# GpSimd no longer waits for VectorE's w_lo in front of x_lo and the identity addition into W2

## The reference

```
x = x + (x @ weight[subject].T + bias[subject])            # L0: 8 subjects, 512 x 512
x = x + rotate(x, amplitudes ** dt, frequencies * dt)      # L1: pairs of tokens are turned and scaled
x = x + (x @ W[category] + b[category])                    # L2: 64 categories, 512 x 512
h = relu(x @ W1[lang] + b1[lang])                          # L3: one of 10 languages, 512 -> 128 -> 512
x = x + layernorm(x + h @ W2[lang] + b2[lang]) * gamma[lang] + beta[lang]
```

## Time and profile before

| what | value |
|---|---|
| median of three runs | 1252.36 us |
| the profiled execution | 1252.07 us |
| its span, first to last instruction | 1250.2 us |
| mean granted TensorE clock, share of full speed | 0.995 |
| TensorE (PE) busy | 94% |
| VectorE (DVE) busy | 79% |
| GpSimd (POOL) busy | 63% |
| ScalarE (ACT) busy | 47% |
| HBM traffic over the span | 232 GB/s |

### The profile page before, as it was taken

One profiled execution on the slowest core, in us unless ns is written; L12 is line 12 of the kernel. 1 busy time (PEld: TensorE's weight loads), 2 busy tenths in 40 slices (PEclk: granted clock), 3 DMA queues, 4 the chain that ended last, 5 costly groups with the idle time before them and its releaser, 6 DMA issues.

```text
span 1250.2 us, 28648 instructions
## 1 busy us (share of the span) xinstructions
PE 1175.2 (94%) x5902; PEld 886.8 (71%) x5902; DVE 990.5 (79%) x1465; ACT 582.2 (47%) x923; POOL 783.6 (63%) x792
## 2 busy tenths in 40 slices
PE   2799999999989999999999999999999999999996
PEld 1667767777767777677777677767776777767774
DVE  3488888888888788888788788788888888778887
ACT  2345445444444444545444445454444544444542
POOL 3966656656666657656666566666656666755654
PEclk9999999999999999999999999999999999999999
DMA  6967776776776678667768676776677687867771
GB/s 246 418 206 237 230 242 204 247 235 203 251 256 221 208 248 277 222 205 232 254 199 268 225 231 205 248 259 219 224 243 251 199 251 240 271 214 222 238 225 59
DMA packets 96410, 291.75 MB, mean 233 GB/s; under 512 B 11584, under 2 KB 11712, under 8 KB 78272
## 3 DMA queue, kind: packets, MB, share of 16 engines
q1 hardware_dynamic: 96192, 289.52, 70.6%
HBM read 255.93 MB, written 33.55 MB: 232 GB/s over the span
## 4 chain that ended last, share of the span: by engine, by line
PE 53%; DVE 24%; issue 12%; DVEq 8%; DMA 1%; POOL 1%; SPq 0%; POOLq 0%; ACT 0%; ACTq 0%
DVE w_lo L630 11%; PE ps_l L752 9%; PE ps_l L784 9%; PE ps_y L813 9%; PE ps_l L747 6%; DVE ps_y L658 5%; DVE stats L660 5%; PE ps_x3T L794 4%; DVEq L202 3%; DVEq L205 3%; PE ps_l L774 3%; PE ps_l L737 3%; PE ps_l L778 3%; PE ps_mix L763 3%; PE ps_hT L804 3%
## 5 line engine op out<-in xcount | busy, mean ns | idle before, releaser
L381 POOL TENSOR_TENSOR x_lo<-x_in,x_hi 128x512 fp32r<-128x512 f32 x128 | 165.5, 1293 | 360.1 <-DVE w_lo L630 356.8
L630 DVE TENSOR_TENSOR w_lo<-w_in,w_hi 128x1024 fp32r<-128x1024 f32 x256 | 304.1, 1229 | 0.0
L486 ACT ACTIVATE w_hi<-w_in 128x1024 fp32r<-128x1024 f32 x256 | 255.2, 1045 | 7.9 <-PE ps_l L778 4.7
L451 ACT ACTIVATE ps_diag<-ident,cos 128x128 f32<-128x128 f32 x128 | 47.6, 372 | 382.1 <-DVE mix L604 381.8
L784 PE MATMUL ps_l<-w_lo,x2T_hi 128*128 128x512 f32 x512 | 174.5, 424 | 19.5 <-DVE w_lo L630 15.2
L405 POOL TENSOR_TENSOR x<-x,beta_sb 128x512 f32<-128x512 f32 x128 | 162.9, 1272 | 28.9 <-POOL x3b L398 28.7
L763 PEld LDWEIGHTS ps_mix<-mix,x 128*128 128x128 f32 x1024 | 133.7, 191 | 63.1 <-issue 58.6
L737 PE MATMUL ps_l<-w_hi,x_hi 128*128 128x512 f32 x512 | 150.5, 416 | 20.1 <-ACT w_hi L462 14.2
L398 POOL TENSOR_TENSOR x3b<-x,bup_sb 128x512 f32<-128x512 f32 x128 | 163.3, 1276 | 8.2 <-DVE x L652 8.2
L375 POOL TENSOR_TENSOR w_in<-w_in,ident 128x512 f32<-128x512 f32 x128 | 165.5, 1293 | 3.9 <-DMA w_in<-W 3.7
L645 DVE TENSOR_TENSOR x2T_lo<-ps_mix,x2T_hi 128x512 fp32r<-128x512 f32 x128 | 88.5, 691 | 99.8 <-issue 94.3
(11 more groups left out here) (82 smaller groups left out, 1647.3 us busy)
## 6 DMA issues: line engine op xcount, KB each, us to landing
w_in<-W SPq DMA_DIRECT2D x128, 1024.0 KB, 5.4
b_in<-b SPq DMA_DIRECT2D x136, 256.0 KB, 5.4
x_in<-xT SPq DMA_DIRECT2D x128, 256.0 KB, 4.5
w_in<-W SPq DMA_DIRECT2D x128, 256.0 KB, 2.7
out<-yb SPq DMA_DIRECT2D x128, 256.0 KB, 4.8
w_in<-W0T SPq DMA_DIRECT2D x8, 1024.0 KB, 5.4
bup_sb<-bup SPq DMA_DIRECT2D x1, 2560.0 KB, 8.9
wup_sb<-Wup SPq DMA_DIRECT2D x1, 2560.0 KB, 11.3
```

Source lines behind the costliest of these rows:

```text
L381: pool.tensor_tensor(x_lo[s % 2][:, :], x_in[s % XB][:, :], x_hi[s % 2][:, :].bitcast(fp32), ALU.subtract).then_inc(x_lo_made, 1)
L486: act.activation(w2_hi[:, halves[n]], w2_in[s % WB][:, halves[n]], ACT.Copy).then_inc(w2_hi_made, 1)
L630: dve.tensor_tensor(w2_lo[:, half], w2_in[s % WB][:, half], w2_hi[:, half].bitcast(fp32), ALU.subtract).then_inc(w2_lo_made, 1)
```

## The change

In GpSimd's loop one line goes: the wait until w2_lo of sample s is complete. x_lo of s+2 still waits for x_hi of s+2, and the identity addition still waits for its W2 to have landed.

```diff
@@ -421,7 +421,6 @@
                 if s >= 2:
                     inverse_deviation(s - 2)
                 if s < LAST - 1:
-                    pool.wait_ge(w2_lo_made, 2 * s + 2)
                     rest_of_x(s + 2)
                     fold_w2(s + 2)
                 lang = language_of(pool, s)
```

## The result

The changed kernel takes 1560.35 us (median of four runs, 1558.38 to 1563.86) against 1251.71 us before: a ratio of 1.247, 95% interval 1.245 to 1.248. It is 309 us slower. The direction and the mechanism were right, the size was not: the forecast of 1478 us, and its range up to 1502, lie 82 and 58 us too low.

A forecast was written before the change was run, and what follows sets the result against it. The prediction took a loop of TensorE and VectorE through w_lo to bound the kernel. Delays of w_lo by GpSimd's additions, 191 + 26 + 9 = 226 us, on 1252.1 gave 1478 us, range 1375 to 1502.

The forecast's parts named there:

- What bounds the kernel: Loop of TensorE and VectorE through w_lo and ps_y, period 9.05 us; w_lo's end moves the period one for one.
- The early start brings nothing: Starting x_lo and the identity addition into W2 earlier on GpSimd gains nothing; costed at +0.
- The price of a step, +2.11 us: In a typical step, GpSimd's two additions delay the end of w_lo's second half from 617.49 to 619.60 us.
- The order that I took from 351 and 492 us: GpSimd and VectorE take turns by instruction: x_lo, w_lo's first half, identity addition, w_lo's second half; +2.11 us a step.
- The rival with VectorE first: w_lo's first half gets in before x_lo, so a typical step costs +1.1 us; 1387 us in all, chance 0.21.
- The sum, +226 us: Whole run: 91 typical steps 191 us, 16 late ones 26, 17 about arrivals of W0 and x 9.
- TensorE's granted clock, 0.995 in the mean, stays: TensorE's clock would not change in the changed kernel, since the waits of W0 had not lowered it; no cost added.
- a clock step: An example of something unseen, with a shifted transfer the other; slower, chance 0.02 together.
- What would show it: Signs: w_lo's mean about 2.1 us, the addition into W2 2.3 us, TensorE's busy share about 80%.

The follow-up runs named there:

- idle statistics: The kernel before, with VectorE delayed by statistics of an unused scratch tile in front of each half of w_lo: two a half 1600.03 us, one 1377.73 us.

## Why the prediction was wrong

- **What bounds the kernel**: right. Every microsecond that w_lo's end moved came out in the period, by a collision or by idle statistics.
- **The early start brings nothing**: right. GpSimd waits 338 us for x3 instead.
- **The price of a step, +2.11 us**: right within 0.02 us. The order that I took from 351 and 492 us (x_lo, first half, identity addition, second half) is that of the typical step. The rival with VectorE first does occur, at 605.77 us for instance, where an addition into W0 had delayed GpSimd; 15 of the 128 first halves were not held up.
- **The sum, +226 us**: 231 at full clock. Right.
- **The step that failed**: "TensorE's granted clock, 0.995 in the mean, stays: the waits of W0 didn't lower it." The term stood at nothing. The clock fell 57 times, at waits of 0.4 and 1.5 us in every step, and that cost 77 us. I had taken single waits of one to two microseconds, each between steps without any, as the measure for that, and overlooked what one of them did. In the kernel before, around and behind the W0 that arrived at 680 us, TensorE waited 1.15, 0.80 and 1.69 us, and 1.6 us behind the end of the last wait the granted clock did fall. Behind the other six arrivals it did not. I gave "a clock step" 0.02 together with everything else unseen, and so the range ended at 1502. That fall in two matmul groups of the kernel before (L752's four usually take 1.09 us), then in a stretch, its columns as above:

```profile
693.35 1.19 PE L778 MATMUL ps_l<-w_hi,x2T_lo 128*128 128x512 f32 x4 [1.69 <-DVE x2T_lo L645]
...
697.49 1.51 PE L752 MATMUL ps_l<-w_lo,x_hi 128*128 128x512 f32 x4
```

```profile
695.00:698.40 3.40, 3.09 (x8) 2.16 (x8) 2.84 (x5) 2.30 (x3) 2.75 (x3) 0.50 0.48 134
```

- **What would show it**: w_lo's mean (2.14 us against some 2.1), the addition into W2 (2.2 to 2.3) and TensorE's busy share (83% against 80%) came as written; the one sign that I had not listed was the length of a matmul.

## What to carry to other kernels

When a wait looks useless because the data are there earlier, ask what it keeps apart: here a VectorE subtraction with two SBUF inputs and a GpSimd addition took turns by whole instructions, and the one that came second paid, even by 0.1 us. When a change makes TensorE wait in every step, forecast two cases, with and without a fall of its clock; here 1.0 us a step was borne and 2.1 us was not, and the falls cost a third of the stall again (77 us on 231). Look in the profile of before for the granted clock behind its longest waits one by one; the mean over the span hides a single fall. A matmul group whose mean time has grown is the sign to look for on the page.

## What I had not expected of the hardware

- A wait of 1.48 us behind one of 0.36, repeated each step, brought the granted clock down in about every second step. 1.0 us a step did not (mean clock 0.995 and 0.988).
- Work that nobody reads, put into TensorE's waits, made the kernel 77 us faster: 1560 to 1483 us, with 232 us of matmuls added.
- GpSimd's occupation is no measure of the harm that it does: a power of 2.27 us and two memsets of 0.53 us beside w_lo left its 1.217 us alone, an addition of 1.29 us cost 1.0. In the other order the power did lose, up to 1.05 us. The page "SBUF — State Buffer" of the Trainium skill ("Who interferes with whom") says that the shared pair is held for the whole instruction; of the power that did not hold here (2.27 us, w_lo at 1.217), nor at 33 us.
